# Expert blocks of a routed feed-forward: gathers four blocks ahead, and scatters released by SyncE instead of by the landing of the one before

## What is computed

```python
probs = softmax(xf @ W_gate)                # 4096 tokens, 16 experts
top_g, top_i = top_k(probs, 2)
for e in range(16):                         # D = 256, H = 512
    y += gates[:, e, None] * (gelu(xf @ W1[e]) @ W2[e])
t = t + y
```

## Time and profile before

| | |
|---|---|
| median of 3 runs | 1165.85 us (1165.17 to 1165.89) |
| profiled execution, its own time | 1161.35 us |
| its span, first to last instruction | 1159.7 us |
| mean granted TensorE clock | 0.938 |
| first scatter begins | 782.41 us |
| last scatter begins | 1154.60 us |
| PE, DVE, ACT, POOL busy, share of the span | 82%, 54%, 39%, 28% |

### The profile page before, as it was taken

How to read it: one execution, slowest core, us unless ns; L and a number is a source line. 1 busy time by engine, 2 the same in 40 slices (tenths; PEclk the granted TensorE clock), 3 DMA queues, 4 the chain that set the end, 5 groups by cost and what they waited for, 6 DMA issues and landing times.

```text
span 1159.7 us, 21335 instructions
## 1 busy us (share of the span) xinstructions
PE 949.3 (82%) x6946; PEld 699.9 (60%) x6947; DVE 620.8 (54%) x1583; ACT 453.8 (39%) x1023; POOL 327.6 (28%) x360
## 2 busy tenths in 40 slices
PE   3899986899986899987899895258888888888876
PEld 2655664655664655664556663147777777777765
DVE  5766676766676766676766678942222222222211
ACT  3523373523373523373523463223333333333331
POOL 2320011220011220011320011335555555555553
PEclk8999997899997899997999997559999999999999
DMA  4000003000003000002000004973333333323330
GB/s 126 2 1 1 1 2 110 2 1 1 1 2 111 1 1 1 1 2 75 1 1 1 1 1 156 266 251 51 53 53 52 51 53 57 51 47 54 52 46 14
DMA packets 41266, 50.87 MB, mean 44 GB/s; under 512 B 10625, under 2 KB 32513, under 8 KB 41185
## 3 DMA queue, kind: packets, MB, share of 16 engines
q0 software_dynamic: 17344, 27.24, 12.1%
q1 hardware_dynamic: 23840, 22.56, 6.5%
HBM read 32.96 MB, written 18.78 MB: 45 GB/s over the span
## 4 chain that ended last, share of the span: by engine, by line
PE 46%; DVE 17%; issue 17%; DMA 13%; ACT 4%; POOL 2%; DVEq 1%; POOLq 0%; ACTq 0%
PE PS L502 9%; DMA out_dram<-low,row_of 7%; PE PS L531 6%; PE PS L905 5%; DMA low<-rows_scratch,token_of 5%; PE PS L896 4%; PE PS L765 4%; DVE neg_max L1118 3%; PE PS L573 3%; PE PS L567 3%; POOL out_dram L415 2%; PE PS L562 2%; PE PS L648 1%; PE PS L667 1%; PE PS L627 1%
## 5 line engine op out<-in xcount | busy, mean ns | idle before, releaser
L905 PE MATMUL PS<-arena,low 128*128 x632 | 156.5, 391 | 37.7 <-ACT low L1064 23.6
L363 POOL TENSOR_SCALAR aggr<-aggr 128x1 f32<-128x1 f32 x64 | 14.6, 228 | 568.9 <-DVE aggr L1180 568.9
L415 POOL DMA_INDIRECT out_dram<-low,row_of x79 | 126.2, 1598 | 158.7 <-DMA out_dram<-low,row_of 83.9
L502 PE MATMUL PS<-ident,arena 128*128 128x128 f32 x1032 | 146.5, 288 | 26.1 <-ACT arena L987 10.6
L896 PEld LDWEIGHTS PS<-low 128*128 128x128 f32 x1264 | 155.6, 194 | 4.5 <-DVE low L1458 0.6
L502 PEld LDWEIGHTS PS<-ident,arena 128*128 128x128 f32 x1032 | 122.5, 149 | 59.4 <-issue 39.2
L896 PE MATMUL PS<-low 128*128 128x128 f32 x1264 | 156.1, 278 | 0.2 <-DVE low L1458 0.2
L905 PEld LDWEIGHTS PS<-arena,low 128*128 128x128 f32 x632 | 113.7, 189 | 66.7 <-issue 54.1
L1118 DVE TENSOR_REDUCE neg_max<-PS 128x1 f32<-128x1024 f32 (+1 forms) x97 | 118.4, 1221 | 48.6 <-PE PS L562 37.0
L1064 ACT ACTIVATE low<-PS 128x512 f32<-128x512 f32 x79 | 47.2, 597 | 222.4 <-PE PS L896 211.6
L973 ACT ACTIVATE arena<-PS,neg_max 128x1024 f32<-128x1024 f32 x64 | 71.4, 1115 | 138.9 <-DVE neg_max L1118 138.9
(11 more groups left out here) (196 smaller groups left out, 1438.1 us busy)
## 6 DMA issues: line engine op xcount, KB each, us to landing
arena<-in_L_ffn_W_dram SPq DMA_DIRECT2D x32, 512.0 KB
arena<-in_x_dram SPq DMA_DIRECT2D x4, 1024.0 KB, 8.2
rows_scratch<-arena POOLq DMA_DIRECT2D x4, 1024.0 KB, 6.6
out_dram<-t POOLq DMA_DIRECT2D x4, 1024.0 KB, 9.1
low<-rows_scratch,token_of POOLq DMA_INDIRECT x79
out_dram<-low,row_of POOLq DMA_INDIRECT x79, 3.8
arena<-in_L_attn_w_qkv_dram SPq DMA_DIRECT2D x1, 768.0 KB, 4.9
arena<-in_L_attn_w_out_dram SPq DMA_DIRECT2D x1, 256.0 KB, 5.4
```

The source lines that it names most:

```text
L415: pool.indirect_dma_start(out_rows, bass.IndirectOffsetOnAxis(ap=row_of[:, n:n + 1], axis=0), y_sb[:, n % 4, :], None, bounds_check=T - 1, ...
L502: mm = pe.transpose(PS[0:s.shape[1], dst_bank, n * P:n * P + s.shape[0]], s, ident[0:s.shape[0], 0:s.shape[0]])
L905: mm = pe.matmul(PS[:, 6 + p, 0:D], hT[:, p, c, :], w2_sb[:, bass.ds(e * (HC * D) + c * D, D)], start=c == 0, stop=c == HC - 1)
```

## The change

Gathers run four blocks ahead. Four are issued before the first block, and `add_rows(n)` issues gather n + 4. Since that one overwrites the buffer of block n itself, GpSimd now also waits until VectorE has taken the gate values of block n (`parts_made`).

GpSimd no longer waits for the landing of scatter n - 1. It waits for `scatter_ok >= n + 1`, and SyncE adds one to `scatter_ok` for each block in order. For blocks 0 to 3 SyncE waits as GpSimd did, for the landing of the block ahead. From block 4 on SyncE waits for the landing of every block ahead of the first block of n's expert (or ahead of block 4, where that is later). How many landings that makes on each of the four semaphores is in a table `release`, made by VectorE from `expert_of`'s source in `first_blocks`; SyncE loads four entries into registers for each block and waits for the four values. The blocks behind the last expert count as one more expert.

```diff
+        block_no = sb("block_no", [P, BW])
+        first_of = sb("first_of", [P, 2, BW])
+        release = sb("release", [P, BW, 4], I32)
...
             def add_rows(n):
-                if n + 3 < BLOCKS:
+                if n + 4 < BLOCKS:
                     pool.wait_ge(xt_mm, n + 1)
-                    gather(n + 3)
+                    pool.wait_ge(parts_made, n + 1)
+                    gather(n + 4)
                 pool.wait_ge(y_copied, n + 3)
 
-                if n >= 1:
-                    pool.wait_ge(y_stored[(n - 1) % 4], ((n - 1) // 4 + 1) * 16)
+                pool.wait_ge(scatter_ok, n + 1)
                 pool.indirect_dma_start(out_rows, ...
...
-            for n in range(3):
+            for n in range(4):
                 gather(n)
...
+            for n in range(4):
+                if n >= 1:
+                    sp.wait_ge(y_stored[n - 1], 16)
+                sp.sem_inc(scatter_ok, 1)
+            sp.wait_ge(release_ready, 1)
+            with sp.Fori(4, BLOCKS) as n:
+                landed = [sp.value_load(release[0:1, bass.ds(n, 1), u:u + 1].rearrange("p o u -> p (o u)"), min_val=16,
+                                        max_val=16 * (ROUNDS + 1)) for u in range(4)]
+                for u in range(4):
+                    sp.wait_ge(y_stored[u], landed[u])
+                sp.sem_inc(scatter_ok, 1)
...
+            dve.tensor_copy(block_no[:], iota_i[:, 0:BW])
...
+            def first_blocks():
+                e = slot[:, 2, :]
+                link(dve.memset(first_of[:, 0, 0:1], 0.0))
+                link(dve.tensor_tensor(first_of[:, 0, 1:BW], e[:, 1:BW], e[:, 0:BW - 1], ALU.not_equal))
+                link(dve.tensor_tensor(first_of[:, 0, :], first_of[:, 0, :], block_no[:], ALU.mult))
+                link(dve.tensor_tensor_scan(first_of[:, 1, :], first_of[:, 0, :], zero_col[:].broadcast_to([P, BW]), 4.0, ALU.max, ALU.add))
+                for u in range(4):
+                    ins = dve.tensor_scalar(release[:, :, u], first_of[:, 1, :], float(3 - u), None, ALU.add)
+                link(ins)
+                dve.tensor_scalar(release[:], release[:], 2, 4, ALU.logical_shift_right, ALU.logical_shift_left).then_inc(release_ready, 1)
...
             rows_turned(0, 0, 0)
             rows_turned(1, 1, 1)
+            first_blocks()
```

More of the change, by code:

```diff
@@ L273, in conv_attn_nystrom_moe_kernel @@
         tables_ready = sem("tables_ready")
+        release_ready = sem("release_ready")
+        scatter_ok = sem("scatter_ok")
         expert_dma = [sem(f"expert_dma{k}") for k in range(2)]
```

## The result

The changed kernel takes **1083.57 us** (median of 4 runs, 1082.36 to 1085.87), the kernel before 1165.51 in the same comparison: a ratio of 0.931, 95% interval 0.9287 to 0.9333, or 81.9 us less. The forecast was 1109 with a range from 1091 to 1136.

A forecast was written before the change was run, and what follows sets the result against it. Two loops, scatter landings and late gathers, set 4.80 us a block. 55 x 3.83 + 16 x 4.8 = 287.5 against 340.1 gains 52.6, plus 4 at the end: 1165.85 - 56.6 = 1109 us, range 1091 to 1136.

The forecast's parts named there:

- Two loops of nearly one period bound the kernel: Expert blocks: scatter to scatter over its landing, 4.6 to 4.7 us; through the gather, 10.1 us for two blocks.
- Gathers four ahead no longer bound, and the 0.75 at L905 goes: Gather's loop spans three blocks, 3.4 us each; PE's register-load gap of 0.75 us between transposes and `rows_out` disappears.
- From a gather's end to the next scatter 0.85: On POOL, scatters inside an expert: taken as 0.85 us, making POOL's cycle 3.74, with one more wait 3.8.
- The cycle gives almost none of it back, so I count every one in full: After a scatter that waits, POOL is about 1 us late and its 3.8 us cycle recovers almost nothing; 16 steps.
- PE's step 3.83: PE's own pace per block, 1.83 + 1.78 + 0.22 us, taken for 55 ordinary steps.
- A waiting step 4.8: Scatters that still wait, 16 steps: landing 3.8, SyncE's relay 0.1, 0.85 to the scatter's start, 4.8 us.
- SyncE's turn 2.8, hidden: SyncE's loop of four register loads and four waits takes 2.8 us a turn, below 3.8, costing only the relay.
- The rival: SyncE's loop becomes the pace above 4.8 us a turn; at 5.5 us 52 us more, 1218 us; chance 0.06.
- One queue serves DMAs in turn: Rival: a DMA begins only when the other has landed, a block takes 4.1 to 5.0 us; 1135 us; chance 0.10.
- The last blocks, gain 4: Scatters 74 to 78, now one expert: about 13 us instead of 17.0, gain 4 us.
- VectorE: Nine added instructions and one of 320 elements, some 2.3 us in an idle stretch, `release_ready` by 776, costing nothing.
- more than forecast: Rival: 0.30 between gather and scatter, POOL's cycle 3.2, all 71 steps at 3.83 us; 1093 us; chance 0.05.

The follow-up runs named there:

- Each part alone: Kernel before with only gathers four ahead added: 1152.22 us; changed kernel with gathers three ahead again, scatters released by SyncE: 1156.05 us.
- the cycle at 3.93: Changed kernel with a memset of 128 x 900 that nobody reads on POOL between each block's gather and the waits: 1106.51 us.

## Why the prediction was wrong

*Two loops of nearly one period bound the kernel.* Right. Each part alone leaves the other loop at 4.71 and 4.73 us a step.

*Gathers four ahead no longer bound, and the 0.75 at L905 goes.* Right in the main: 0.22 between transposes and `rows_out` in the changed kernel, and the run without the register load shows what the 0.75 was. It comes back in a few blocks behind a late gather, and gathers five ahead take some 4 us more off.

*From a gather's end to the next scatter 0.85.* **This is the step that failed.** It is 0.30. The bounds were both in the prediction (0.30 from a gather behind a scatter, 1.06 from above), and I chose near the upper one, because after every release the trace before shows 0.77 to the scatter's start. That 0.77 runs from the register move in POOL's queue ahead of the scatter. In the trace before every scatter was waited for, so it always lay open. Where the waits are already satisfied, it passes while the gather still runs. The chain after shows it:

```profile
1056.72 0.26 POOL low L409
1056.98 0.04 issue
1057.02 0.03 POOLq L420
1057.05 0.55 issue
...
1058.01 3.76 DMA out_dram<-low,row_of
```

The gather starts at 1056.72 and runs until 1057.71; the scatter's register move is issued at 1057.02, inside it. So a scatter starts 0.76 to 0.77 behind the end of its move or 0.30 behind the instruction ahead, whichever is later; that holds within 0.1 us for 73 of the 79 scatters. POOL's cycle is 1.60 + 0.30 + 0.99 + 0.30 = 3.20 us, not 3.8.

*"The cycle gives almost none of it back, so I count every one in full."* This falls with the cycle. POOL can recover up to 3.73 - 3.20 = 0.53 us a step. The 16 waiting steps took 72.8 us together, forecast 76.8; the 55 others took 195.5, a mean of 3.55 and so less than PE's own step, forecast 210.7. With the cycle at 3.93 nothing is recovered, as I had said.

*PE's step 3.83.* This term was mis-sized too: it is 3.73. I had added the times of a stalled block, whose `rows_out` takes 1.83; the block behind it in the earlier trace rows already shows the form of 1.89 that leads to 1.73. Over 71 steps this is 7.1 us. At PE's step the 71 steps would take 264.8, and measured are 268.3. So of the 16 x 0.97 = 15.5 us that I had charged for the waits 3.5 are left. That is the remainder of a subtraction and no count of its own, but it is near the 4 us that a fifth block of lead takes off.

*A waiting step 4.8.* Nine of the 16 took 4.49 to 4.74 (4.71 above), but they run from 3.73 to 5.58, with a mean of 4.55. *SyncE's turn 2.8, hidden.* It is 3.0 and hidden. The Trainium skill's floor of 600 ns for a register load (DMA: Bandwidth & Descriptors, § Latency and other measured facts) is about what a load costs here with its register work, 0.64, but not what the load alone takes, 0.27. The turn of 4.0 by it did not come. The rival stands as a mechanism, though: two loads more and SyncE is the pace. *One queue serves DMAs in turn.* Not seen: scatter 72 starts 3.19 behind scatter 71, with a gather between them, and lands in 3.76. *The last blocks, gain 4.* 4.7. *Scatters 0 to 3 keep their pace.* They gained 1.3.

*VectorE.* `first_blocks` has nine instructions in all, not nine and one. It ran from 776.22 to 778.17, later than the forecast 776 but in an idle stretch, and cost nothing.

*From the sum to the time.* Between the two profiled executions the kernel gained 75.5 us, 18.9 more than the forecast 56.6. The other 6.4 of the miss lie in how far each profiled execution is from its median: I took a gain read from one execution off a median.

*The range.* The rival "more than forecast" had this very mechanism, with a chance of 0.05 and a time of 1093, on PE's 3.83. With 3.73 it gives 1086, and measured are 1083.57. I let the low end of the range rest on one bound and not on both, and gave little weight to a price for which the nearest row of a satisfied wait, 0.30, spoke.

## What to carry over

When two loops hold a pipeline at nearly the same period, each fix tried alone looks nearly worthless; work out the period of every loop, with the number of blocks that it spans, before judging one. An instruction's start cost read from rows that all end a wait is an upper bound: where the wait is gone, the queue may spend it under the instruction ahead. A helper queue that hands out permissions needs a turn shorter than the new step, not the old one.

## What the runs showed of the hardware

- A scatter on POOL that was waited for started 0.77 us behind its register move, 0.84 behind the landing that released it. If its waits had passed it started 0.30 behind the gather ahead, and 0.17 behind a memset.
- A register load on PE with its register work, behind a late gather, held up a group of multiplications by 0.7 us, in rows that name another engine as releaser. Without it the kernel before ran 9.9 us faster.
- TensorE left the routing at a granted clock of 0.50 (1.2 GHz). It was still there up to 780.20 where it had stood still for 0.59 us ahead of each `hidden`, and rose to the 2.4 GHz level between 776.40 and 778.80 where it had worked without a break from 772.74.
- Scatter 73 starts 1.66 us behind its register move in the changed kernel and 1.64 in the kernel before (the earlier trace rows has its 3.39 us under "issue"), where most need 0.77. After SyncE's release at 1061.79 it starts at 1063.59. In all 13 profiled executions it starts 5.4 to 6.3 us behind scatter 72. In both executions of the changed kernel scatters 37 and 54 are late in the same way (1.7 and 2.1). No run here tried the cause.
